# One half of each unit's sixteen small transfers moves from SyncE's queue to GpSimd's

## The chip, the cores and the metric

The kernel runs on one core of one Trainium2 chip. The metric is the time of one execution on the device in microseconds (us). Before the change the median of three runs is 1092.51 us (1091.69 to 1094.83).

## The reference

The reference is a two-layer transformer stack on 2048 tokens of 256 features. Layer 0 is a 16-head softmax attention over all 2048 tokens followed by a mixture of eight experts (two per token) beside a shared one; layer 1 is a small ReLU attention followed by a linear map. Each of the four steps stands behind a layer norm with modulation and adds into x. The change touches the softmax attention of layer 0 alone:

```
q, k, v = (x @ Wq + bq, x @ Wk + bk, x @ Wv + bv)      # 2048 x 16 heads x 16
scores  = einsum('bnhd,bmhd->bnmh', q, k) / sqrt(16)
att     = softmax(scores, axis=2)                      # over the 2048 keys
attval  = einsum('bnmh,bmhd->bnhd', att, v)
```

## The kernel before

**Units.** The attention is done in NU = 16 units: four chunks of 512 queries, and for each of them four groups of four heads. Unit u has two sides. Its maxima: for each query and head the largest score over all keys, found by TensorE (`maxima`, L627; matmuls at L634) and VectorE (`reduce_pair`, reductions at L1433). Its scores: TensorE multiplies keys with queries again (L658), ScalarE takes the exponential (L1147), and TensorE weighs the values (L689). The maximum is subtracted inside the second matmul: it is written as two float16 rows (a rounded value and its remainder, NM = 2) under the query's 48 rows in `qst`, against constant rows in `kst`. So a unit's scores can't begin before its maxima lie in `qst`.

**Order.** Each unit has MT = 16 steps t. In a step TensorE does, interleaved, the maxima of a later unit, the four scores of its own and the weighing of the step before. The maxima run LEAD = 5 steps ahead: steps 0 to 10 of unit u finish the maxima of unit u+1, steps 11 to 15 begin those of unit u+2. After step 10 VectorE takes `negative_max` (L1437) and transposes it (`turn_max`, L1444), GpSimd splits it (`split_max`, L1992: nms, nmp, nmp, the last at L1999 raises `nm_s`), and SyncE's `store_max` (L375, transfers at L383) brings it from `nmp` into `qst` in sixteen transfers of 8 rows x 32 numbers, 0.5 KB each: two halves of heads b (rows 0 to 63 and 64 to 127 of `qst`), two parts m, four blocks q. Each raises `nm_in` by 16 on landing. At the head of unit u TensorE waits for all of them (`unit`, L638). Unit 0 alone has its second half begun by ScalarE (L1125).

**SyncE's queue.** For v = 4 to 15 it does in turn: `load_q` for unit v, `move_attention(v-3)` (16 transfers, L393, after GpSimd's `gate_attention`, L2034 and L2037), waits for `nm_s`, `store_max` for unit v-1, waits until these have landed, then `zero_slots` (L417), and for v = 4 the large weight loads before it, for v = 15 `load_down` (L410). A wait in this queue holds back all that stands behind it. For v = 2 and 3 it is the same without the loads at the end. The maxima of unit 15 are stored after the loop.

**GpSimd's queue.** It adds the residual to x in two halves of eight tiles (`residual`, L2014), with `split_max(1)` between them; then for each unit `gate_attention(u)`, `split_max(u+2)`, `add_attention(u)` (L2045). Ahead of `split_max(15)` it has the work on the expert weights: `down_gated` (L2076, when `load_down` has landed) and `down_rounded` (L2103, L2105). Its indirect transfers (L2164, L2194) come after the attention.

**Other names.** `qst` has four slots, so unit v takes the slot of unit v-4. TensorE's matmuls of maxima go to two pairs of PSUM banks, and wait for VectorE's reduction of the pair before the last.

Of the kernel before, what the change touches and what calls it, by code (L numbers as in the profile page):

```python
# [21 lines left out]
TPC = CH // P  # L22
H, DH = 16, 16
G = 4
NG = H // G
NU = NC * NG
MT = T // P
HALF = 64
BLK = 3
KR = BLK * DH  # L30
NM = 2
# [3 lines left out]
GP = G // 2  # L35
LOADS = 2 * BLK
# [26 lines left out]
MI = G * TPC  # L63
QD = 32
NQ = P // QD
MAX_LOADS = 2 * NM * NQ
ROW_UNIT = 2.0 ** 15


def build(nc, x_in, wq, bq, wk, bk, wv, bv, routerT, gate_w, up_w, down_w, sg_w, sg_b, su_w, su_b,  # L70
# [18 lines left out]
    with ctx:  # L89
# [21 lines left out]
        nms, nmp = new("nms", [P, QD]), new("nmp", [P, NM, QD], F16)  # L111
# [138 lines left out]
        def sem(name):  # L250
            names[name] = ctx.enter_context(nc.semaphore(name))
            return names[name]
# [13 lines left out]
        slot_out = [sem(f"slot_out{n}") for n in range(SLOTS)]  # L266
        v_ps, v_s, vb_s, vconst = sem("v_ps"), sem("v_s"), sem("vb_s"), sem("vconst")
        kst_in = [sem(f"kst_in{g}") for g in range(3)]
        kst_one, q_in, nm_in = sem("kst_one"), sem("q_in"), sem("nm_in")
        mx_ps, mx_read, nmx_s = sem("mx_ps"), sem("mx_read"), sem("nmx_s")  # L270
        nmT_s, nm_step, nm_s = sem("nmT_s"), sem("nm_step"), sem("nm_s")
        sc_ps, p_s, pv_s, o_s = sem("sc_ps"), sem("p_s"), sem("pv_s"), sem("o_s")
# [70 lines left out]
        def _(sp):  # L343
# [28 lines left out]
                                     qd[Q_PART[r]].rearrange("(h b d) n -> b d h n", b=2, d=DH)[b][  # L372
                                         :, GP * g:GP * (g + 1), bass.ts(c, CH)]).then_inc(q_in, 16)

            def store_max(slot, halves=range(2)):  # L375

                for b in halves:
                    for m in range(NM):
                        row = HALF * b + KR + m
                        rows = qst[row:row + 1, slot, 0:GP, :].rearrange("p k (j n) -> p (k j) n", j=TPC)  # L380
                        for q in range(NQ):
                            at_ = QD * q + MI // 2 * b
                            sp.dma_start(rows[:, :, QD * q:QD * (q + 1)],  # L383
                                         nmp[at_:at_ + MI // 2, m, :]).then_inc(nm_in, 16)

            def move_attention(u, heads=range(G)):

# [59 lines left out]
            load_k(3, kst_in[2])  # L447
            store_items(EASY, max(n for which, n in FILL[:BEFORE] if which == "i") + 1)
            sp.wait_ge(nm_s, 1)
            store_max(0, (0,))  # L450
            store_items(min(n for which, n in FILL[BEFORE:] if which == "i"), len(ITEMS))
            sp.wait_ge(nm_in, 16 * MAX_LOADS)
            for v in range(2, G):
                load_q(v, 0)
                sp.wait_ge(q_in, 16 * LOADS * (v + 1))
                if v >= G - 1:
                    move_attention(v - G + 1)
                sp.wait_ge(nm_s, v)
                store_max(v - 1)
                sp.wait_ge(nm_in, 16 * MAX_LOADS * v)  # L460
            for v in range(G, NU):
                c, g = v // NG, v % NG
                if v == G:
                    stored(sp, range(len(ITEMS) - SLOTS, len(ITEMS)))
                sp.wait_ge(sc_ps, G * MT * (v - NG + 1))
                load_q(g, c)
                sp.wait_ge(q_in, 16 * LOADS * (v + 1))
                move_attention(v - G + 1)
                sp.wait_ge(nm_s, v)
                store_max((v - 1) % NG)  # L470
                sp.wait_ge(nm_in, 16 * MAX_LOADS * v)
                if v == G:
                    load_shared(ffw_in[0])
                    sp.wait_ge(vb_s, MT // 2)
                    load_gate_up(ffw_in[1])
                    sp.wait_ge(zero_s, 1)
                zero_slots(ZERO_TILES * (v - G), min(ZERO_TILES * (v - G + 1), TS))
                if v == NU - 1:
                    sp.wait_ge(sc_ps, G * MT * (NU - NG + 1))
                    load_down(ffw_in[2])  # L480
# [51 lines left out]
        def _(pe):  # L532
# [104 lines left out]

            def unit(u, g, ahead, first=False, beside=None, banks=(4, 5, 6)):  # L638

                pe.wait_ge(nm_in, (u + 1) * (16 * MAX_LOADS))  # L640
                for t in range(MT):
                    run = (t + LEAD < MI and ahead >= 1) or (t + LEAD >= MI and ahead >= 2)
                    nxt = t + LEAD < MI
                    i = (t + LEAD) % MI
                    v, vg = (u + 1, (g + 1) % NG) if nxt else (u + 2, (g + 2) % NG)
                    if run and i == 0:
                        pe.wait_ge(q_in, (u + 3) * (16 * LOADS))
                    pairs = v * (2 * MI) + 2 * i

                    def score(k):  # L650
                        n = G * t + k
                        bank = banks[n % len(banks)]
                        if n >= len(banks):
                            pe.wait_ge(p_s, u * (G * MT) + n - len(banks) + 1)
                        elif n == 0 and not first:
                            pe.wait_ge(p_s, u * (G * MT))
                        rows = slice(HALF * (k % 2), HALF * (k % 2) + KR + NM)
                        nc.tensor.matmul(ps[:, bank, :], kst[rows, GP * g + k // 2, P * t:P * (t + 1)],  # L658
                                         qst[rows, g, k // 2, :], start=True, stop=True).then_inc(sc_ps, 1)

                    def next_maxima(p):
                        if run:
                            maxima(vg, i, p, pairs + p)

                    def weigh_before(half):
                        if t == 0 and not first:
                            weigh((g - 1) % NG, MT - 1, half)
                        if t >= 1:
                            if half == 0:
                                pe.wait_ge(p_s, u * (G * MT) + G * t)  # L670
                                if t == 1 and not first:
                                    pe.wait_ge(o_s, u)
                            weigh(g, t - 1, half)

                    next_maxima(0)
                    score(0)
                    score(1)
                    weigh_before(0)
                    next_maxima(1)
                    score(2)  # L680
                    score(3)
                    weigh_before(1)
                    if beside:
                        beside(t)
# [1240 lines left out]
        def _(pool):  # L1925
# [66 lines left out]
            def split_max(v):  # L1992

                pool.wait_ge(nmT_s, v + 1)
                pool.wait_ge(nm_in, v * (16 * MAX_LOADS))
                nc.gpsimd.tensor_scalar(nms[:], nmT[:], 1.0 / ROW_UNIT, None, ALU.mult).then_inc(nm_step, 1)  # L1996
                nc.gpsimd.tensor_scalar(nmp[:, 0, :], nmT[:], 1.0 / ROW_UNIT, None, ALU.mult).then_inc(nm_step, 1)
                pool.wait_ge(nm_step, 2 * (v + 1))
                nc.gpsimd.tensor_tensor(nmp[:, 1, :], nms[:], nmp[:, 0, :], ALU.subtract).then_inc(nm_s, 1)  # L1999

            for f, (which, n) in enumerate(FILL):
# [8 lines left out]
                else:  # L2010
                    residue(n)


            def residual(lo, hi):  # L2014
                for t in range(lo, hi):
                    then(nc.gpsimd.tensor_scalar(xt[:], x[:, t, :], mv0[:, t, 0:1], rs0[:, t:t + 1],  # L2016
                                                 ALU.subtract, ALU.mult))
                    then(nc.gpsimd.tensor_tensor(xt[:], xt[:], rows0[:, GCA, :], ALU.mult))
                    then(nc.gpsimd.tensor_tensor(xt[:], xt[:], rows0[:, GSA, :], ALU.add))
                    then(nc.gpsimd.tensor_tensor(x[:, t, :], x[:, t, :], xt[:], ALU.add))  # L2020
# [19 lines left out]
            def add_attention(u):  # L2040

                c, g, w = u // NG, u % NG, G * DH
                pool.wait_ge(att_in, 16 * G * NQ * (u + 1))
                dst = x[:, c * TPC:(c + 1) * TPC, w * g:w * (g + 1)]
                nc.gpsimd.tensor_tensor(dst, dst, att_t[:].rearrange("p j k d -> p j (k d)"), ALU.add).then_inc(att_s, 1)  # L2045
# [3 lines left out]
            gates_by_head()  # L2049
            split_max(1)  # L2050
            pool.wait_ge(nm_s, 2)
            residual(NT // 2, NT)

            def zeros():
# [70 lines left out]
            for u in range(NU - 1):  # L2125
                if u == NU - 2:
                    input_rest(0)
                    tokens_by_row(0)
                    deviation(1, 1)
                gate_attention(u)  # L2130
                if u == 0:
                    zeros()
                if u == 5:
                    shared_rounded()
                if u == 6:
                    router_constants()
                    sort_tables()
                if u == NU - 3:
                    down_rounded()
                    deviation(1, 0)  # L2140
                if u + 2 < NU:
                    split_max(u + 2)
                    pool.wait_ge(nm_s, u + 3)
                add_attention(u)
                pool.wait_ge(att_s, u + 1)
                if u == NU - 4:
                    down_gated()
# [118 lines left out]
```

## Time and profile before

| | |
|---|---|
| median of three runs | 1092.51 us |
| profiled execution | 1092.85 us |
| its span | 1091.0 us |
| busy, share of the span | TensorE 87%, VectorE 78%, ScalarE 62%, GpSimd 27% |
| mean granted TensorE clock | 0.916 |
| L1433 (VectorE, maxima) | 512 reductions, 597.4 us busy, 1216 ns each |
| L1147 (ScalarE, exponentials) | 1024, 553.5 us busy, 595 ns each |

Times are of one profiled execution and count from the start of its span. PE is TensorE, PEld its weight loads, DVE VectorE, ACT ScalarE, POOL GpSimd; SPq, ACTq and POOLq are the issue of transfers by an engine. A busy TensorE is not one at its peak, since its matmuls are pipelined. The granted clock is a share of the full one, 2.4 GHz. Idle time of an engine matters where it lies in the chain that ends last.

### The profile page before, as it was taken

Reading aid. Unit: us, or ns where it says so; the run is one execution under the profiler, and the core shown is the slowest. Engines: PE = TensorE matmul, PEld = TensorE weight load, DVE = VectorE, ACT = ScalarE, POOL = GpSimd, SP = SyncE. Lnnn points to the kernel's source line nnn. Section 1 sums busy time; section 2 is a strip of 40 time slices with the busy share of each in tenths; the row PEclk is TensorE's granted clock in tenths of the full one; section 3 lists DMA queues with packets and bytes.
Section 4 is the critical chain, followed back from the end, with each engine's and each line's share of the span. In section 5 each row is a group of like instructions: output and inputs, shape, how many; then the busy total and the mean of one; then the engine's idle time right before and its main releaser. Section 6 shows DMA issues by size and latency. Waiting matters only on the chain.

```text
span 1091.0 us, 22102 instructions
## 1 busy us (share of the span) xinstructions
PE 944.5 (87%) x7744; PEld 426.7 (39%) x7744; DVE 856.0 (78%) x1204; ACT 674.9 (62%) x1300; POOL 296.8 (27%) x351
## 2 busy tenths in 40 slices
PE   4887989899899989999899898995969989797766
PEld 3442223223222222222232232222347778696545
DVE  6589979889889999899898898892537755746665
ACT  0222879779788888798797797794744334354112
POOL 2052894001000221100100010074435720314453
PEclk9999889989899998899998898898888989898888
DMA  7470000023110101001101001120001253343221
GB/s 174 120 127 30 18 9 6 13 70 110 30 27 9 30 12 25 28 6 33 28 6 33 28 6 31 37 34 2 6 6 55 81 160 99 92 135 108 59 67 58
DMA packets 90477, 54.81 MB, mean 50 GB/s; under 512 B 49334, under 2 KB 86038, under 8 KB 90390
## 3 DMA queue, kind: packets, MB, share of 16 engines
q1 hardware_dynamic: 82806, 43.52, 16.1%
q0 software_dynamic: 3072, 8.39, 2.5%
q10 hardware_dynamic: 4512, 1.67, 0.8%
q8 instruction: 63, 1.03, 0.4%
q14 instruction: 24, 0.20, 0.1%
HBM read 28.63 MB, written 22.54 MB: 47 GB/s over the span
## 4 chain that ended last, share of the span: by engine, by line
PE 29%; DVE 23%; issue 14%; SPq 13%; POOL 11%; DMA 5%; ACT 2%; ACTq 1%; DVEq 0%; POOLq 0%
DVE mxp L1433 14%; SPq L383 12%; PE ps L689 5%; PE ps L886 4%; PE ps L634 3%; PE ps L658 2%; PE ps L912 2%; DMA qst<-nmp 2%; PE ps L569 2%; POOL xt L2016 2%; PE ps L580 2%; DMA yg<-y_slots,slots 1%; PE ps L971 1%; PE ps L787 1%; DMA d_raw<-down_w 1%
## 5 line engine op out<-in xcount | busy, mean ns | idle before, releaser
L1433 DVE TENSOR_REDUCE mxp<-ps 128x2 f32<-128x1024 f32 x512 | 597.4, 1216 | 56.6 <-PE ps L634 55.4
L1147 ACT ACTIVATE prob<-ps 128x512 f32<-128x512 f32 x1024 | 553.5, 595 | 135.7 <-PE ps L658 102.9
L689 PE MATMUL ps<-prob,vp 128*32 128x256 f32 x4096 | 348.1, 414 | 14.6 <-ACT prob L1147 1.4
L634 PE MATMUL ps<-kst,qst 48*128 48x512 f16 x1024 | 211.3, 410 | 45.0 <-DMA qst<-nmp 34.8
L658 PE MATMUL ps<-qst,kst 50*128 50x512 f16 x1024 | 210.2, 404 | 10.3 <-DMA qst<-nmp 10.3
L689 PEld LDWEIGHTS ps<-prob,vp 128*32 128x32 f32 x4096 | 83.3, 111 | 202.1 <-ACT prob L1147 101.9
L634 PEld LDWEIGHTS ps<-kst,qst 48*128 48x128 f16 x1024 | 49.6, 93 | 274.4 <-issue 141.6
L658 PEld LDWEIGHTS ps<-qst,kst 50*128 50x128 f16 x1024 | 87.8, 96 | 50.6 <-ACT prob L1147 12.3
L2034 POOL TENSOR_TENSOR att_u<-o_x,rec 128x256 f32<-128x256 f32 x16 | 9.9, 620 | 255.6 <-DVE rec L1457 255.4
L1996 POOL TENSOR_SCALAR nms<-nmT 128x32 f32<-128x32 f32 x16 | 4.8, 300 | 209.8 <-DVE nmT L1444 193.7
L1690 DVE TENSOR_TENSOR hdt<-ps,sgt 128x176 f32<-128x176 f32 x46 | 15.6, 338 | 48.3 <-ACT sgt L1211 46.9
L2194 POOL DMA_INDIRECT yg<-y_slots,slots x32 | 32.1, 1002 | 51.3 <-DMA y_slots<-ysb 30.5
L1211 ACT ACTIVATE sgt<-ps 128x176 f32<-128x176 f32 x46 | 14.6, 317 | 49.4 <-PE ps L886 49.4
L886 PE MATMUL ps<-gu_hi,th 128*128 x92 | 35.8, 389 | 1.6 <-issue 1.0
L900 PE MATMUL ps<-ident,hdt 128*88 128x128 f32 x92 | 18.8, 288 | 17.3 <-DVE hl L1694 17.3
L912 PE MATMUL ps<-d_hi,hh 88*128 x92 | 31.4, 341 | 2.4 <-issue 2.4
L1319 DVE TENSOR_SCALAR xh<-x,mv,rs 128x256 f32<-128x256 f32 x56 | 20.8, 433 | 16.0 <-POOL rs L1949 12.4
L2164 POOL DMA_INDIRECT x_slots<-h_tmA,slots x24 | 26.8, 1116 | 18.4 <-DVE slots L1576 11.5
L886 PE MATMUL ps<-gu_lo,th 128*128 x92 | 30.9, 336 | 0.0
L886 PE MATMUL ps<-gu_hi,tl 128*128 x92 | 30.7, 334 | 0.0
L1217 ACT ACTIVATE hh<-ps 88x256 fp32r<-88x256 f32 x46 | 17.5, 381 | 19.0 <-PE ps L900 18.8
L1224 ACT ACTIVATE ysb<-ps 128x256 f32<-128x256 f32 x46 | 17.7, 384 | 18.4 <-PE ps L912 18.4
(271 smaller groups left out, 1151.1 us busy)
## 6 DMA issues: line engine op xcount, KB each, us to landing
xg<-x_slots SPq DMA_DIRECT2D x46, 128.0 KB, 2.1
y_slots<-ysb SPq DMA_DIRECT2D x46, 128.0 KB, 1.9
x_slots<-zero SPq DMA_DIRECT2D x10, 512.0 KB, 3.0
qst<-nmp SPq DMA_DIRECT2D x248, 0.5 KB
att_t<-att_u SPq DMA_DIRECT2D x248, 8.0 KB, 1.8
qst<-q_parts SPq DMA_DIRECT2D x96, 32.0 KB, 1.9
kst<-k_parts SPq DMA_DIRECT2D x24, 128.0 KB, 5.2
x<-x SPq DMA_DIRECT2D x4, 512.0 KB, 9.2
```

What stands on the lines that cost most here:

```text
L383: sp.dma_start(rows[:, :, QD * q:QD * (q + 1)], nmp[at_:at_ + MI // 2, m, :]).then_inc(nm_in, 16)
L569: last = nc.tensor.matmul(ps[:, 4 + n % 2, :], w[:, k, P * ft:P * (ft + 1)], hT[:, k, CH * c:CH * (c + 1)], start=k == 0, stop=k == KT - 1)
L580: last = nc.tensor.matmul(ps[:, 6 + i % 2, D * j:D * (j + 1)], hT[:, k, P * (2 * i + j):P * (2 * i + j + 1)], wv_sb[:, k, :], start=k == 0 ...
L634: last = nc.tensor.matmul(ps[:, 2 * p + b, :], qst[rows, g, a, P * j:P * (j + 1)], kst[rows, GP * g + a, CH * m:CH * (m + 1)], start=True, ...
L658: nc.tensor.matmul(ps[:, bank, :], kst[rows, GP * g + k // 2, P * t:P * (t + 1)], qst[rows, g, k // 2, :], start=True, stop=True).then_inc ...
L689: last = nc.tensor.matmul(ps[VW * k:VW * (k + 1), 7, own], vp[:, g, t, k, :], prob[:, t % 2, k, own], start=t == 0 and half == 0, stop=t = ...
L886: last = nc.tensor.matmul(ps[:, 2 + i % 2, 0:2 * I], a[:, i % 2, k, :], b[:].rearrange("p e k n i -> p (e k n i)")[:, bass.ds(e * GW + k * ...
L912: last = nc.tensor.matmul(ps[:, 6, 0:D], a[:, i % 2, n, :], b[:].rearrange("p e n d -> p (e n d)")[:, bass.ds(e * (2 * D) + n * D, D)], st ...
L1147: nc.scalar.activation(prob[:, t % 2, k, :], ps[:, banks[(G * t + k) % len(banks)], :], ACT.Exp, scale=exp_scale).then_inc(p_s, 1)
L1433: nc.vector.tensor_reduce(own, ps[:, 2 * p:2 * p + 2, :], AX.X, ALU.max).then_inc(mx_read, 1)
L2164: nc.gpsimd.indirect_dma_start(x_slots[part], bass.IndirectOffsetOnAxis(ap=slots[:, PARTS[part][0] + t, k:k + 1], axis=0), h_tm[part][:, t ...
L2194: nc.gpsimd.indirect_dma_start(yg[:, m % 4, :], None, y_slots[part], bass.IndirectOffsetOnAxis(ap=slots[:, TPC * d + j, k:k + 1], axis=0)) ...
```

## The change: what it does

`store_max` on SyncE now begins only the eight transfers of the first half (rows 48 and 49 of `qst`). GpSimd has a `store_max(v)` of its own for the second half (rows 112 and 113), right behind `split_max(v)` and its wait for `nm_s`, ahead of `add_attention` (for unit 1, ahead of the second half of the residual). Its eight raise a new semaphore, `nm_low_in`. TensorE's unit waits for both; `split_max` waits for both before it overwrites `nmp`; SyncE goes on when its own eight have landed. Unit 0 keeps ScalarE's eight. The number of transfers, their sizes and addresses stay.

```diff
-MAX_LOADS = 2 * NM * NQ
+MAX_LOADS = NM * NQ
...
-            def store_max(slot, halves=range(2)):
-                for b in halves:
-                    for m in range(NM):
-                        row = HALF * b + KR + m
...
+            def store_max(slot):
+                for m in range(NM):
+                    rows = qst[KR + m:KR + m + 1, slot, 0:GP, :].rearrange("p k (j n) -> p (k j) n", j=TPC)
+                    for q in range(NQ):
+                        sp.dma_start(rows[:, :, QD * q:QD * (q + 1)],
+                                     nmp[QD * q:QD * q + MI // 2, m, :]).then_inc(nm_in, 16)
...
-                sp.wait_ge(nm_in, 16 * MAX_LOADS * v)
+                sp.wait_ge(nm_in, 16 * MAX_LOADS * (v + 1))
...
-                pe.wait_ge(nm_in, (u + 1) * (16 * MAX_LOADS))
+                pe.wait_ge(nm_in, (u + 2) * (16 * MAX_LOADS))
+                if u:
+                    pe.wait_ge(nm_low_in, u * (16 * MAX_LOADS))
...
-                pool.wait_ge(nm_in, v * (16 * MAX_LOADS))
+                if v:
+                    pool.wait_ge(nm_in, (v + 1) * (16 * MAX_LOADS))
+                if v >= 2:
+                    pool.wait_ge(nm_low_in, (v - 1) * (16 * MAX_LOADS))
...
+            def store_max(v):
+                pool.wait_ge(q_in, 16 * LOADS * (v + 1))
+                for m in range(NM):
+                    row = HALF + KR + m
+                    rows = qst[row:row + 1, v % NG, 0:GP, :].rearrange("p k (j n) -> p (k j) n", j=TPC)
+                    for q in range(NQ):
+                        at_ = QD * q + MI // 2
+                        pool.dma_start(rows[:, :, QD * q:QD * (q + 1)],
+                                       nmp[at_:at_ + MI // 2, m, :]).then_inc(nm_low_in, 16)
...
             split_max(1)
             pool.wait_ge(nm_s, 2)
+            store_max(1)
             residual(NT // 2, NT)
...
                     split_max(u + 2)
                     pool.wait_ge(nm_s, u + 3)
+                    store_max(u + 2)
                 add_attention(u)
```

## Rows read from the trace of the kernel before

**Rows 1.** The page's part 4: the chain that ended last, by line.

```profile
DVE mxp L1433 14%; SPq L383 12%; PE ps L689 5%; PE ps L886 4%; PE ps L634 3%; PE ps L658 2%; PE ps L912 2%; DMA qst<-nmp 2%; PE ps L569 2%; POOL xt L2016 2%; PE ps L580 2%; DMA yg<-y_slots,slots 1%; PE ps L971 1%; PE ps L787 1%; DMA d_raw<-down_w 1%
```

**Rows 2.** Waits of PE: us in total, times, longest; 200 to 703, then the span.

```profile
PE ps L634 <- DMA qst<-nmp: 27.7, 12, 2.7
...
PE ps L658 <- DMA qst<-nmp: 10.3, 1, 10.3
```

**Rows 3.** Timeline (start, us, [idle before <- releaser]): POOL, then SP, before unit 4.

```profile
310.97 0.29 POOL L1996 TENSOR_SCALAR nms<-nmT 128x32 f32<-128x32 f32 x1 [17.65 <-DVE nmT L1444]
...
311.59 0.25 POOL L1999 TENSOR_TENSOR nmp<-nms,nmp 128x32 f16<-128x32 f32 x1
...
311.87 10.79 SPq L383 DMA_DIRECT2D qst<-nmp  x16
```

**Rows 4.** Timeline of PE at the head of unit 4.

```profile
321.02 0.64 PE L689 MATMUL ps<-prob,vp 128*32 128x256 f32 x8
323.76 0.61 PE L634 MATMUL ps<-kst,qst 48*128 48x512 f16 x2 [2.10 <-DMA qst<-nmp]
```

**Rows 5.** Timeline of DVE, unit 3 and the head of unit 4.

```profile
291.66 18.72 DVE L1433 TENSOR_REDUCE mxp<-ps 128x2 f32<-128x1024 f32 x16
310.42 0.22 DVE L1437 TENSOR_REDUCE nmx<-mxp 128x16 f32<-128x64 f32 x1
...
310.81 11.37 DVE L1433 TENSOR_REDUCE mxp<-ps 128x2 f32<-128x1024 f32 x10
324.41 1.23 DVE L1433 TENSOR_REDUCE mxp<-ps 128x2 f32<-128x1024 f32 x1 [2.23 <-PE ps L634]
...
327.85 0.72 DVE L1453 STREAM_TRANSPOSE o_x<-ps 128x512 f32<-128x512 f32 x1 [0.24 <-PE ps L689]
```

**Rows 6.** Windows of unit 4: us, busy time (instructions) by engine, granted clock, DMA share.

```profile
323.70:331.70 8.00, 7.90 (x52) 1.52 (x52) 5.61 (x6) 4.34 (x8) 0.00 (x0) 0.59 0.33 92
331.70:366.00 34.30, 31.49 (x332) 9.90 (x332) 32.77 (x31) 30.39 (x56) 2.86 (x6) 1.00 0.05 5
```

**Rows 7.** Timeline of POOL's indirect transfers, and DVE beside the first.

```profile
840.10 2.11 POOL L2164 DMA_INDIRECT x_slots<-h_tmA,slots  x1 [0.30 <-DVE h32a L1504]
...
880.12 0.96 POOL L2164 DMA_INDIRECT x_slots<-h_tmB,slots  x1 [0.30 <-issue]
...
839.76 1.61 DVE L1625 TENSOR_TENSOR gu_lo<-gu_raw,gu_hi 128x1408 fp32r<-128x1408 f32 x1
```

**Rows 8.** DMA issues: count, KB each, median us to landing; span, span, then 238 to 256.

```profile
x_slots<-h_tmA,slots POOLq DMA_INDIRECT x24, 2.4
...
qst<-q_parts SPq DMA_DIRECT2D x96, 32.0 KB, 1.9
...
qst<-q_parts SPq DMA_DIRECT2D x6, 32.0 KB, 2.9
```

**Rows 9.** Timeline before unit 2: POOL, SP, PE.

```profile
173.57 0.73 POOL L2037 TENSOR_TENSOR att_u<-att_u,ga_q 128x256 f32<-128x256 f32 x1
...
174.37 10.60 SPq L393 DMA_DIRECT2D att_t<-att_u  x16
185.02 10.82 SPq L383 DMA_DIRECT2D qst<-nmp  x16
...
196.90 0.48 PE L634 MATMUL ps<-kst,qst 48*128 48x512 f16 x2 [2.57 <-DMA qst<-nmp]
```

**Rows 10.** The chain in order of time before unit 15 (start, us), then PE's timeline.

```profile
690.83 0.71 SPq L383
...
703.61 12.19 DMA d_raw<-down_w
715.93 8.88 POOL d_raw L2076
...
741.16 0.70 SPq L383
...
753.05 0.61 PE L658 MATMUL ps<-qst,kst 50*128 50x512 f16 x2 [10.25 <-DMA qst<-nmp]
```

More of the change, by code:

```diff
@@ L268, in build @@
         kst_in = [sem(f"kst_in{g}") for g in range(3)]
-        kst_one, q_in, nm_in = sem("kst_one"), sem("q_in"), sem("nm_in")
+        kst_one, q_in, nm_in, nm_low_in = sem("kst_one"), sem("q_in"), sem("nm_in"), sem("nm_low_in")
         mx_ps, mx_read, nmx_s = sem("mx_ps"), sem("mx_read"), sem("nmx_s")
@@ L373, in load_q @@
                                          :, GP * g:GP * (g + 1), bass.ts(c, CH)]).then_inc(q_in, 16)
-            def store_max(slot, halves=range(2)):
-                for b in halves:
-                    for m in range(NM):
-                        row = HALF * b + KR + m
[L380 to L384, printed above, removed]
+            def store_max(slot):
[4 more added lines that the diff above has]
+                                     nmp[QD * q:QD * q + MI // 2, m, :]).then_inc(nm_in, 16)
             def move_attention(u, heads=range(G)):
@@ L449, in _ @@
             sp.wait_ge(nm_s, 1)
-            store_max(0, (0,))
+            store_max(0)
             store_items(min(n for which, n in FILL[BEFORE:] if which == "i"), len(ITEMS))
-            sp.wait_ge(nm_in, 16 * MAX_LOADS)
+            sp.wait_ge(nm_in, 16 * MAX_LOADS * 2)
             for v in range(2, G):
@@ L470, in _ @@
                 store_max((v - 1) % NG)
-                sp.wait_ge(nm_in, 16 * MAX_LOADS * v)
+                sp.wait_ge(nm_in, 16 * MAX_LOADS * (v + 1))
                 if v == G:
```

## The prediction

> **What bounds the kernel now.** I read the page's chain of waits first, because the busy shares can't tell which of four half-busy engines sets the end. The chain has VectorE's reductions of maxima at 14% and, right behind, SyncE issuing the small transfers (L383) at 12% [rows 1]: some 130 us in which the end waits for nothing but issue. The second view is the list of waits: between 200 and 703 TensorE stands 27.7 us in 12 waits for these transfers, 2.3 us each, at the heads of units 3 to 14, and once 10.3 us at the head of unit 15 [rows 2].
>
> The third view is the timeline around one such head, unit 4. GpSimd's last split ends at 311.84, SyncE issues sixteen transfers in 10.79 us (0.674 us apart, the last beginning at 321.98) [rows 3], and TensorE starts the unit at 323.76 [rows 4]. From the split to the start that is 11.92 us, of which 1.78 us lie behind the start of the last transfer. TensorE's work of the unit before ended at 321.66 [rows 4]. So the transfers have a **budget** of 321.66 - 311.84 = 9.82 us in which they cost nothing, and they overrun it by 2.1 us here. VectorE sees the same hole as 2.23 us [rows 5].
>
> The hole costs more than its length. In the 8 us behind it the granted clock is 0.59, so most of them at the lower level of 1.2 GHz; in the remaining 34.3 us it is 1.00 [rows 6]. At the low clock TensorE doesn't keep VectorE fed.
>
> What comes next if the hole goes? VectorE's own work of a unit: 32 reductions at 18.72/16 = 1.17 us are 37.4, the small maximum and its transposition put 0.39 between two reductions (310.42 to 310.81), the transposition of the output 0.72, its wait 0.24 [rows 5]: 38.8, and I take 38.9 us, for the reciprocal and seams. The unit takes 366.0 - 323.7 = 42.3 [rows 6]. **At most 3.4 us a unit can be had**: 2.1 of hole, 1.3 of slow clock. Then VectorE is the bound.
>
> **The change part by part.**
>
> *SyncE's half.* Eight issues go from its queue: 8 x 0.674 = 5.4 us. Its own eight are in place 7 x 0.674 + 1.78 = 6.5 us after the split, 3.3 inside the budget. The waits on other semaphores have the same meaning and cost nothing.
>
> *GpSimd's half.* The trace shows no plain transfer begun by GpSimd. Call the distance between two of them p, and L the time from the start of the last to its landing: the half is in place after 0.1 + 7p + L (0.1 for the two semaphore waits, as between 311.84 and 311.87 on SyncE, rounded up). The nearest row is GpSimd's indirect transfer: 0.96 us and a gap of 0.30 ahead of it, p = 1.26 [rows 7]; it lands after 2.4 us [rows 8]. From below, SyncE's 0.674 for the same transfer: were GpSimd quicker still, SyncE's half would be the last, so less brings no more. From above, the slowest indirect transfer, 2.11 + 0.30 = 2.41 [rows 7]. I take p = 1.1: the gap whole, and 0.8 of the 0.96, since eight rows of 64 bytes have to be described and not 128 rows. L is 2.4: the landing writes less, but shares the engines, as told below. So the half needs 0.1 + 7.7 + 2.4 = 10.2 us, 0.4 over the budget.
>
> Only a page has a price for the plain transfer: the Trainium skill, "DMA: Bandwidth & Descriptors", section "Latency and other measured facts", gives about 1 us to the first byte where GpSimd's software writes the descriptors and about 0.6 where hardware does; SyncE's 0.674 is near the second, the first is shown by no run here. By 1.0 for p, an estimate from that page, the half would fit the budget and the sum would come to about 1051 us.
>
> *Heads of units 3 to 13, eleven of them.* Each loses 3.4 us but keeps 0.4 of hole, on which I count no fall of the clock: 11 x (3.4 - 0.4) = 33.0 us gained (the slow stretch of unit 13 is in it, which lies ahead of the split for unit 14).
>
> *Neighbours.* SyncE goes on when its own half has landed, at 6.5 us, and then begins 0.5 MB of zeros and six loads of queries, which before came behind the last maximum. They now run beside GpSimd's last transfers. Loads of queries take 2.9 us to land beside heavy traffic and 1.9 otherwise [rows 8]; the 2.4 in L has part of that. At the head of unit 3, where the weights of the experts are loaded, I add 1 us once.
>
> *Ahead of unit 2.* GpSimd's eight issues for unit 1 push the second half of the residual back by 8p = 8.8 us. That half is not covered: gate_attention follows it and ends at 174.30, SyncE's move_attention begins at 174.37 and takes 10.6 us, and only behind that come the maxima of unit 2 at 185.02 [rows 9]. So SyncE's queue is 8.8 us late and then 5.4 us shorter: unit 2 starts 3.4 us later. That unit 1 starts sooner helps nothing, since unit 2 waits for this queue. TensorE waited 2.57 here [rows 9]; this hole grows.
>
> *Ahead of unit 15.* Here GpSimd is the chain: SyncE's store for unit 14 (690.83), load_down landing for 12.19 us behind its issue, GpSimd's 8.88 us on it and the rest up to 741.16, and the store for unit 15, 11.9 us up to 753.05 [rows 10]. load_down waits for SyncE's half alone and so begins 5.4 us sooner; GpSimd's own eight are done by then. The last store takes 10.2 and not 11.9. Together 7.1 us gained, and TensorE, which waited 10.25 us, still waits.
>
> *Covered by GpSimd's idle time.* In units 2 to 13 its eight issues (8.8 us) stand ahead of add_attention, and behind that GpSimd waits about 17 us and more for VectorE [rows 3]. If this cover went, move_attention would come late, as ahead of unit 2.
>
> *Sum.* +3.4 - 33.0 + 1.0 - 7.1 = -35.7 us. The profiled execution took 1092.85 us (span 1091.0, 1.85 around it), 0.3 above the median of 1092.51. 1092.85 - 35.7 = **1057 us**.
>
> **The rivals.**
>
> *GpSimd pays the price of its indirect transfers.* With p = 1.26 and L = 2.4 the half needs 11.3 us, and 1.5 of the hole stay: 0.8 x 11 = 8.8 gained at the heads, 4.7 lost ahead of unit 2, 5.4 + 0.6 gained ahead of unit 15, 10 in all: 1083, if the clock still falls; with the clock kept, 14 less, 1069. For it speaks that this is the one measured row of GpSimd's queue; against it that those transfers have sixteen times as many rows.
>
> *GpSimd's half becomes the later one than all sixteen were: slower.* The place is the same eight issues, ahead of every head and ahead of the residual. All terms together change by 92 us for one us of p (8 ahead of unit 2, 77 at the heads, 7 at unit 15), and with L = 2.4 they are zero at p = 1.37. At p = 1.5 and L = 2.6 the half takes 13.2 us: +6.6, +1.1 x 11, -5.4 + 1.3, together +15: 1108. For it: p = 1.37 is only 0.11 above the indirect row. Against it: eight rows instead of 128.
>
> *VectorE holds GpSimd up.* One indirect transfer took 2.11 us while VectorE ran a subtraction with both inputs in SBUF (from 839.76) [rows 7]. At p = 2.41 the half takes 19.4 us, the holes grow by 7.3 x 11, unit 2 starts 13.9 later, unit 15's stage loses 2.1: about 1189. Against it: in the 12 us behind a split VectorE does ten reductions out of PSUM and nothing else [rows 5]. The Trainium skill, "SBUF — State Buffer", section "Who interferes with whom", says that a VectorE instruction in certain modes shuts GpSimd out of writing descriptors, and that a reduction never does; by that rule this rival falls, and no run here has shown it yet.
>
> *A small hole still lets the clock fall.* Then 1.3 x 11 = 14 us come back: 1071. The hole of 2.1 us ahead of unit 4 is followed by the slow stretch [rows 6]; a hole of 0.4 us I don't have to read.
>
> **How the numbers follow.** The forecast, with p up to about 1.15, has 0.52; its own range is 1044 (p as on SyncE: 37.4 + 10.8 gained, nothing lost ahead of unit 2) to 1064. The indirect price or the falling clock, 1064 to 1089, has 0.28. No gain, 1089 to 1096, has 0.05; the slow GpSimd 0.12; VectorE's hold 0.03. The range 1042 to 1090 leaves out the last three and a little at the low end, about 0.2. Some 0.3% (3.3 us) is what a measurement of this kernel can tell from no change: faster 0.80, same 0.05, slower 0.15.
>
> **What would show it.** In the profile after: L383 with half its count, on POOL eight transfers behind L1999 some 1.1 us apart; TensorE's waits for the maxima at the heads of units 3 to 14 near zero, the granted clock at 1.00 through them, and a unit of about 39 us; move_attention(0) beginning some 9 us later, near 183; d_raw landing 5.4 us sooner behind the split for unit 14. It is wrong where GpSimd's transfers stand 1.3 us apart or more, where the unit stays above 41 us, or where GpSimd's own queue turns up in the chain of units 3 to 13.

## The result, and the profile after

The changed kernel takes 1041.41 us (median of four runs, 1040.90 to 1042.52); beside it the kernel before took 1092.1. The ratio is 0.9548, with a 95% interval of 0.95 to 0.9595. Ratios here are taken over the fast runs and not from the medians, which leaves out one run of the kernel before beside e1, e2, e3 and e5, and two of e9's six, its profiled one (1038.83) among them. The forecast of 1057 had the sign and the mechanism, but the gain is 51 us and not 36. The median lies 0.6 us under the low end of the wide range, 1042 to 1090 (0.9548 of the 1092.51 that the prediction started from is 1043.1, just inside it), and under the 1044 at which the forecast's own range began. The profiled execution took 1042.52 us (span 1040.7).

The chain that ended last, from the page of the changed kernel, answers to [rows 1]. SyncE's line of the small transfers (12% before) is gone from the list, and VectorE's has fallen from 14% to 3%; TensorE and ScalarE stand there in turn:

```profile
PE ps L688 14%; ACT prob L1146 13%; PE ps L631 8%; PE ps L657 7%; PE ps L885 4%; DVE mxp L1432 3%; PE ps L566 2%; PE ps L911 2%; PE ps L577 2%; PE ps L970 1%; PE ps L786 1%; DMA yg<-y_slots,slots 1%; PE ps L541 1%; SPq L390 1%; DVE x L1745 1%
```

TensorE's waits for the maxima over the whole span (us in total, times, longest) answer to [rows 2]: only the heads of unit 2 and of unit 15 are left.

```profile
PE ps L631 <- DMA qst<-nmp: 6.2, 1, 6.2
...
PE ps L657 <- DMA qst<-nmp: 3.0, 1, 3.0
```

The timelines behind one split (GpSimd, then SyncE) answer to [rows 3]. Under them stand GpSimd's eight per unit as a group (ns: shortest, median, longest; first and last start) and the landing of the transfers out of nmp, us from issue (shortest, median, longest), which the trace has for GpSimd's:

```profile
303.69 0.25 POOL L2001 TENSOR_TENSOR nmp<-nms,nmp 128x32 f16<-128x32 f32 x1
304.23 4.17 POOL L2024 DMA_DIRECT2D qst<-nmp  x8 [0.30 <-POOL nmp L2001]
...
303.96 5.44 SPq L380 DMA_DIRECT2D qst<-nmp  x8
...
L2024 POOL DMA_DIRECT2D qst<-nmp x120: 497/518/824, 143.6 to 699.0; - x120
...
DMA to landing us min/median/max: 1.5/1.9/2.9
```

GpSimd's transfers stand 4.17/8 = 0.52 us apart and were forecast at 1.1. GpSimd's half is in place 0.3 + 7 x 0.52 + 1.9 = 5.8 us behind the split, SyncE's half 6.5, both far inside the budget of 9.8.

The windows of one unit (us, busy time by engine, granted clock, DMA share, GB/s) answer to [rows 6]: 38.57 us and not 42.3, the clock at 1.00 throughout.

```profile
264.57:303.14 38.57, 36.76 (x388) 11.45 (x384) 38.19 (x37) 34.67 (x66) 7.04 (x15) 1.00 0.11 24
```

Ahead of unit 2 (GpSimd, SyncE, TensorE) nothing is won and nothing lost; the rows answer to [rows 9]:

```profile
178.69 0.73 POOL L2050 TENSOR_TENSOR att_u<-att_u,ga_q 128x256 f32<-128x256 f32 x1
...
179.50 10.93 SPq L390 DMA_DIRECT2D att_t<-att_u  x16
190.47 5.46 SPq L380 DMA_DIRECT2D qst<-nmp  x8
...
196.99 0.61 PE L631 MATMUL ps<-kst,qst 48*128 48x512 f16 x2 [6.17 <-DMA qst<-nmp]
```

Ahead of unit 15 (SyncE, GpSimd, SyncE, TensorE), answering to [rows 10], the way from SyncE's store for unit 14 to TensorE's start has shrunk from 62.2 us (690.83 to 753.05) to 50.9 (651.06 to 701.94):

```profile
651.06 5.45 SPq L380 DMA_DIRECT2D qst<-nmp  x8
...
658.00 1.08 SPq L407 DMA_DIRECT2D d_raw<-down_w  x2
...
669.89 8.89 POOL L2090 TENSOR_TENSOR d_raw<-d_raw,rows 88x4096 f32<-88x4096 f32 x1 [13.64 <-DMA d_raw<-down_w]
...
695.16 5.45 SPq L380 DMA_DIRECT2D qst<-nmp  x8
...
701.94 0.39 PE L657 MATMUL ps<-qst,kst 50*128 50x512 f16 x2 [3.03 <-DMA qst<-nmp]
```

**Where the 50.3 us of span came from.** Up to the start of unit 2: +0.1 (196.90 to 196.99). From there to the store for unit 14: 493.9 before, 454.1 now, -39.9. From that store to the start of unit 15: -11.3. From there to the end: 338.0 before, 338.8 now, +0.8.

### The profile page after: what moved, and what is told of

Same layout as the page of the kernel before. It is cut to its first block, busy times and chain, and to the rows that moved or that the text cites. A ratio compares the mean times of both kernels' runs of the same rounds, so it can differ in the third digit from the quotient of the medians.

```text
span 1040.7 us, 22104 instructions
## 1 busy us (share of the span) xinstructions
PE 917.2 (88%) x7744; PEld 427.6 (41%) x7744; DVE 852.5 (82%) x1204; ACT 674.3 (65%) x1300; POOL 358.8 (34%) x471
## 4 chain that ended last, share of the span: by engine, by line
PE 49%; ACT 14%; issue 12%; DVE 12%; POOL 7%; DMA 2%; SPq 1%; ACTq 1%; DVEq 0%; POOLq 0%
PE ps L688 14%; ACT prob L1146 13%; PE ps L631 8%; PE ps L657 7%; PE ps L885 4%; DVE mxp L1432 3%; PE ps L566 2%; PE ps L911 2%; PE ps L577 2%; PE ps L970 1%; PE ps L786 1%; DMA yg<-y_slots,slots 1%; PE ps L541 1%; SPq L390 1%; DVE x L1745 1%
## 5 line engine op out<-in xcount | busy, mean ns | idle before, releaser
L688 PE MATMUL ps<-prob,vp 128*32 128x256 f32 x4096 | 333.4, 398 | 23.1 <-ACT prob L1146 10.0
L631 PE MATMUL ps<-kst,qst 48*128 48x512 f16 x1024 | 202.4, 393 | 16.6 <-DVE mxp L1432 10.4
L657 PE MATMUL ps<-qst,kst 50*128 50x512 f16 x1024 | 201.6, 387 | 6.7 <-ACT prob L1146 3.7
L2024 POOL DMA_DIRECT2D qst<-nmp x120 | 62.8, 531 | 4.5 <-POOL nmp L2001 4.5
```

Source lines behind the costliest of these rows:

```text
L631: last = nc.tensor.matmul(ps[:, 2 * p + b, :], qst[rows, g, a, P * j:P * (j + 1)], kst[rows, GP * g + a, CH * m:CH * (m + 1)], start=True, ...
L688: last = nc.tensor.matmul(ps[VW * k:VW * (k + 1), 7, own], vp[:, g, t, k, :], prob[:, t % 2, k, own], start=t == 0 and half == 0, stop=t = ...
L2024: pool.dma_start(rows[:, :, QD * q:QD * (q + 1)], nmp[at_:at_ + MI // 2, m, :]).then_inc(nm_low_in, 16)
```

## The experiments

The budget theory says that the transfers cost only what they overrun the time between the split and the end of TensorE's work, and the slow clock behind the hole. The rivals were that every transfer taken from SyncE is worth the same, or that GpSimd's share matters for itself. e1 to e5 and e8 differ from the change only in which engine begins which transfer, or in cutting some transfers in two, with `ALL_STORES` the sixteen in the order of the kernel before. This table has the median times (e4, e6 and e10 have a single run each; the kernel before took 1092.2 to 1093.4 beside the experiments), and from each profile the start of unit 15 and what lies between it and the end of the span (us):

| | time | unit 15 starts | from there to the end |
|---|---|---|---|
| before | 1092.1 | 753.05 | 338.0 |
| the change (8 + 8) | 1041.4 | 701.94 | 338.8 |
| e1, 12 + 4 | 1054.6 | 708.59 | 345.8 |
| e2, 14 + 2 | 1061.8 | 716.26 | 347.6 |
| e3, SyncE's cut in two | 1075.9 | 729.47 | 346.3 |
| e4, GpSimd's cut in two | 1079.9 | 729.81 | 348.3 |
| e5, units 14 and 15 alone | 1082.0 | 736.16 | 344.1 |
| e6, half reductions | 1036.1 | 696.58 | 337.7 |
| e7, store first | 1035.3 | 695.23 | 340.2 |
| e8, 0 + 16 | 1056.5 | 715.47 | 340.4 |
| e9, load_down early too | 1032.5 | 690.12 | 346.9 |
| e10, half maxima | 1014.9 | 673.06 | 340.0 |

The last column moves by 10 us among kernels whose code behind the attention is the same. So each experiment is judged by the middle column and the units, not by the time alone; I come back to it. The middle column has a spread of its own: the first small maximum, ahead of all that was changed, starts between 97.3 and 100.7 us in the profiles whose maxima are whole.

**e1: twelve on SyncE, four on GpSimd.**

```diff
-SyncE: ALL_STORES[:8]     GpSimd: ALL_STORES[8:]
+SyncE: ALL_STORES[:12]    GpSimd: ALL_STORES[12:]
```

> SyncE keeps twelve of the sixteen transfers, GpSimd takes four. Budget theory (the transfers cost only what they overrun the 9.82 us between the split and the end of TensorE's work, and the slow clock behind that): twelve on SyncE are in place after 0.05 + 11 x 0.674 + 1.78 = 9.2 us, inside the budget, so the heads of units 3 to 13 keep their whole gain (41 us in the changed kernel); unit 2 starts 0.3 sooner than before the change, load_down 2.7 sooner, the last store 2.7 shorter: some 46 us under the kernel before, 1046, and no waits at those heads. Rival (each transfer taken off SyncE is worth the same share of the 50 us): 4/8 of it, 25 us, 1067.

Windows of one unit, and the head in it (TensorE's timeline):

```profile
266.75:305.34 38.59, 36.66 (x386) 11.46 (x384) 38.19 (x37) 34.68 (x65) 5.02 (x11) 1.00 0.10 24
...
277.18 0.39 PE L655 MATMUL ps<-kst,qst 48*128 48x512 f16 x2 [0.38 <-DMA qst<-nmp]
```

Half as many transfers moved, and the unit is the same 38.6 us: this is the budget theory, and the rival of equal worth (1067) falls. Ahead of unit 15 the way is 55.9 us (652.7 to 708.6), 5.0 longer than in the change, where 5.4 was expected. Unit 15 starts 44.5 us sooner than before, for 46 forecast. The time itself, 1054.6 (ratio 0.9649, 0.9584 to 0.9714), misses 1046 by 8.6 us, 7 of which are in the last column; these belong to neither of the two theories.

**e2: fourteen and two.**

```diff
+SyncE: ALL_STORES[:14]    GpSimd: ALL_STORES[14:]
```

> SyncE keeps fourteen, GpSimd takes two. Budget theory: 0.05 + 13 x 0.674 + 1.78 = 10.6 us, a hole of 0.8 us at the heads of units 3 to 14. If so small a hole leaves the clock at its upper level: 41 - 0.8 x 11 = 32 gained there, 2.7 ahead of unit 15: 1057. If the clock falls behind it as behind the holes of 2.1 us, 1.3 x 11 more is lost: 1071. Rival (same worth for each transfer): 2/8 of 50, 12 us, 1080.

One unit, the head in it, and the 8 us behind that head:

```profile
305.10:344.10 39.00, 36.66 (x388) 11.38 (x387) 38.19 (x37) 34.68 (x65) 4.00 (x9) 1.00 0.11 24
...
315.92 0.39 PE L655 MATMUL ps<-kst,qst 48*128 48x512 f16 x2 [0.79 <-DMA qst<-nmp]
...
315.90:323.90 8.00, 7.23 (x76) 2.21 (x76) 7.51 (x7) 6.22 (x12) 0.00 (x0) 1.00 0.31 92
```

The hole is 0.79 us, as worked out, and the clock stays at its upper level behind it. Three of the twelve heads have more, 1.23 to 1.45 us, and behind these too the clock is 1.00. The unit grows by 0.4 and not by 0.8: half of so small a hole is taken back. Unit 15 starts 36.8 us sooner than before, for 35 forecast in the time; the time, 1061.8 (ratio 0.9712, 0.9658 to 0.9766), is 4.8 over the 1057, with 8.9 us more in the last column than the change has.

**e3: SyncE's eight cut in two, GpSimd's as in the change.**

```diff
+SyncE: in_two(ALL_STORES[:8])    GpSimd: ALL_STORES[8:]
+# in_two: (b, m, q) as rows 0 to 3 and rows 4 to 7
```

> GpSimd does its eight as in the change; SyncE's eight are each cut into two of half the rows, so that it issues sixteen again, of half the bytes. Budget theory with a fixed price per issue: SyncE's share is again in place after 11.9 us, all holes are back, the residual is still 4.5 us late ahead of unit 2, load_down gains nothing: 1092 + 4 = 1097. If the issue goes by rows and not by transfers, or if the gain came from GpSimd's share alone, the time stays at that of the change, 1041 to 1043.

SyncE's sixteen, two heads, and the 8 us behind each of these heads:

```profile
271.95 9.93 SPq L404 DMA_DIRECT2D qst<-nmp  x16
...
282.93 0.39 PE L655 MATMUL ps<-kst,qst 48*128 48x512 f16 x2 [1.90 <-DMA qst<-nmp]
323.16 0.39 PE L655 MATMUL ps<-kst,qst 48*128 48x512 f16 x2 [1.26 <-DMA qst<-nmp]
...
282.90:290.90 8.00, 7.91 (x68) 2.04 (x72) 6.82 (x7) 5.51 (x11) 0.00 (x0) 0.79 0.29 92
323.10:331.10 8.00, 7.20 (x76) 2.22 (x76) 7.47 (x7) 6.18 (x12) 0.00 (x0) 1.00 0.31 92
```

Half the rows cost 0.62 us each where the whole cost 0.67: SyncE's price is nearly one per transfer. GpSimd's share is in place early, and the holes are back nevertheless: 1.26 us at most heads, with units of 39.45, and behind the one of 1.90 the clock falls. It also falls, to 0.58, behind one of 1.56 (unit 13, which takes 41.7 us), but not behind one of 1.58 (unit 10). The rival that GpSimd's share brings the gain (1041 to 1043) falls. The time is 1075.9 (0.9851, 0.98 to 0.9901), not the 1097 expected: I had put the price at the full 0.674 and the hole at 2.1. With 0.62 the same sum gives 0.05 + 15 x 0.62 + 1.78 = 11.1 us and a hole of 1.3, and most holes of 1.3 don't bring the slow clock.

**e4: GpSimd's eight cut in two, SyncE's as in the change.**

```diff
+SyncE: ALL_STORES[:8]    GpSimd: in_two(ALL_STORES[8:])
```

> The change, with each of GpSimd's eight transfers cut into two of half the rows; SyncE's eight as they are. If GpSimd's price is one per transfer, they stay 0.52 us apart, the share is in place after 0.3 + 15 x 0.522 + 1.9 = 10.0 us, 0.2 over the budget, and units stay at 38.6 to 38.7 us, with unit 2 some 3 us later: 1043 to 1050. If the price goes by rows, they stand 0.26 us apart and the time is that of the change, 1041.

GpSimd's group and its landing, as above, its timeline at the ninth burst, and TensorE's waits at the heads, whose releaser the profile doesn't name:

```profile
L2049 POOL DMA_DIRECT2D qst<-nmp x240: 497/518/824, 143.5 to 728.1; - x120
...
DMA to landing us min/median/max: 1.5/1.9/7.7
...
474.67 8.25 POOL L2049 DMA_DIRECT2D qst<-nmp  x16 [3.40 <-issue]
...
PE ps L655 <- issue: 24.1, 13, 6.0
```

Four rows cost what eight cost, 0.52 us: one price per transfer here too. But units 3 to 13 are 38.8 to 42.6 us, the way ahead of unit 15 is 59.3 us (670.5 to 729.8) against 50.9 in the change, and the time is 1079.9 (a single run), far over the 1043 to 1050 forecast. GpSimd's last transfers are now issued when SyncE, whose half was in place at 6.5 us, has begun its zeros and loads. At the heads of units 4 to 6 the slowest of them lands 2.9 to 3.2 us after its issue, where the sum had 1.9; at unit 14, beside load_down, the last three take 6.9 to 7.7 us, and the head waits 6.0 us. In the change no landing takes over 2.9 us: GpSimd is done before SyncE goes on. This looks like the neighbours' term that the prediction feared; that the traffic is the cause is read from the order of the transfers, and no run here moves SyncE's zeros and loads alone. The burst for unit 9 began 3.4 us late for another reason, told below.

**e5: the change for units 14 and 15 alone.**

```diff
+SyncE:  ALL_STORES[:8] if w >= NU - 2 else ALL_STORES
+GpSimd: ALL_STORES[8:] if w >= NU - 2 else []
```

> The change for the stores of units 14 and 15 alone; units 1 to 13 are stored as before. Budget theory with load_down as a term of its own: load_down begins 5.4 us sooner, the last store is 5.4 us shorter, the hole ahead of unit 14 goes: about 11 to 14 us, 1079 to 1082. Rival (all stores alike): 2/15 of 50 us, 7 us, 1085.

```profile
736.16 0.61 PE L681 MATMUL ps<-qst,kst 50*128 50x512 f16 x2 [3.36 <-DMA qst<-nmp]
```

That is TensorE's head of unit 15. SyncE's store for unit 14 began at 684.9, so the way is 51.2 us, against 62.2 before and 50.9 in the change: the 11 us ahead of unit 15 are a term of their own, load_down and the shorter last store. The time, 1082.0 (0.9899, 0.987 to 0.9929), is 10 us under the kernel before, at the upper end of the 1079 to 1082 expected.

**e6 and e10: is VectorE the bound of the changed kernel?** e6 reduces only half of each bank; e10 also computes only that half.

```diff
-nc.vector.tensor_reduce(own, ps[:, 2 * p:2 * p + 2, :], AX.X, ALU.max)
+nc.vector.tensor_reduce(own, ps[:, 2 * p:2 * p + 2, 0:CH // 2], AX.X, ALU.max)
...
-kst[rows, GP * g + a, CH * m:CH * (m + 1)]          # e10
+kst[rows, GP * g + a, CH * m:CH * m + CH // 2]
```

> The change, with VectorE's reductions of maxima reading only half of each bank (256 of 512 columns), so that half of the keys are left out of the maxima. If VectorE's reductions are what sets the changed kernel's unit of 38.57 us, the unit falls to what ScalarE's 64 exponentials need, 64 x 0.54 = 34.6 us or a little more, and the run is about 45 us shorter, 990 to 1000. If it is the round of TensorE and ScalarE that the chain of waits names, the unit stays at 38.5 and the time at 1041.

> As the run with half the reductions (unit 38.30 us), and TensorE's matmuls of maxima take only 256 of each 512 keys too, so that half of the maxima's work is left out on both engines. If the round of TensorE and ScalarE that the chain of waits names (weigh 0.64, maxima 0.32, scores 0.26, exponential 0.60 and the gaps: 2.35 us a step) sets the unit, each step loses about half of the 0.32 and the unit falls by 16 x 0.1 to 0.16, to 35.7 to 36.7 us; ScalarE's 64 exponentials alone need 34.6. If it is something else (the number of waits, ScalarE's own queue), it stays at 38.3.

One unit of e6, then one of e10:

```profile
300.50:338.80 38.30, 36.75 (x388) 11.46 (x384) 23.27 (x36) 34.67 (x65) 7.04 (x14) 1.00 0.11 24
```

```profile
291.90:328.60 36.70, 34.43 (x388) 10.31 (x384) 23.25 (x36) 34.62 (x65) 7.04 (x14) 1.00 0.12 25
```

VectorE's work fell from 38.2 to 23.3 us a unit and the unit by 0.3: VectorE was not the bound, or at most by these 0.3. With half of the matmuls gone too the unit falls to 36.7. The chain of waits in order of time (start, us) shows why, first the change, then e10, one step each:

```profile
280.79 0.60 ACT prob L1146
281.39 0.04 issue
281.44 0.64 PE ps L688 x8
282.07 0.32 PE ps L631 x2
282.40 0.26 PE ps L657 x2
...
282.79 0.35 issue
283.14 0.60 ACT prob L1146
```

```profile
281.45 0.60 ACT prob L1146
282.05 0.04 issue
282.09 0.64 PE ps L688 x8
282.73 0.21 PE ps L631 x2
282.95 0.26 PE ps L657 x2
...
283.35 0.35 issue
283.69 0.60 ACT prob L1146
```

A step is one round of TensorE and ScalarE: exponential, weighing, maxima, scores, next exponential. It takes 2.35 us in the change and 2.24 in e10, and the maxima's part of it went from 0.32 to 0.21. The 16 steps of a unit at 0.11 each are 1.8 us, and the unit fell by 1.6 from e6 to e10. Two reductions of 1.17 us fill the same 2.35 by coincidence.

**e7 and e9: what the profile after points to.** e7 stores unit 2's maxima ahead of move_attention(0). e9 also begins load_down ahead of SyncE's wait for unit 14's maxima, and puts GpSimd's deviation of the layer norm behind the store for unit 15 (the old place of load_down and the move of the deviation are not in the lines shown).

```diff
 sp.wait_ge(q_in, 16 * LOADS * (v + 1))          # v = 2, 3
-if v >= G - 1:
-    move_attention(v - G + 1)
 sp.wait_ge(nm_s, v)
 store_max(v - 1)
+if v >= G - 1:
+    move_attention(v - G + 1)
...
 move_attention(v - G + 1)                       # e9, v = 4 to 15
+if v == NU - 1:
+    sp.wait_ge(sc_ps, G * MT * (NU - NG + 1))
+    load_down(ffw_in[2])
 sp.wait_ge(nm_s, v)
```

> The change, and in SyncE's queue for v = 3 alone the store of unit 2's maxima ahead of move_attention(0) (before, they wait behind its sixteen transfers, and TensorE waits 6.2 us at the head of unit 2). Theory: the maxima of unit 2 are then in place 6.5 us behind the split, before TensorE has ended unit 1; the hole of 6.2 us and some 1 us of slow clock go: 7 us under the change, 1034. Rival: the later move_attention(0) holds GpSimd (add_attention, then gate_attention(1)) and the 7 us come back at the heads of units 3 and 4: 1041.

> As the one before, and ahead of unit 15: load_down begins before SyncE's wait for the maxima of unit 14 and not behind their store, and GpSimd splits and stores unit 15's maxima before the deviation of the layer norm. Theory (GpSimd's work on the expert weights is what unit 15's store waits for): it is done some 13 us sooner, the split waits for VectorE alone, and the hole of 3.0 us at the head of unit 15 shrinks to under 1: 2 to 3 us under the kernel before it, 1031 to 1032. Rival: the deviation, now behind the store, holds back the transposition at the end of unit 14, and nothing is gained: 1034.

SyncE's timeline of e7; then of e9 GpSimd's on the weights and TensorE's head of unit 15:

```profile
182.15 5.34 SPq L380 DMA_DIRECT2D qst<-nmp  x8
187.53 11.43 SPq L390 DMA_DIRECT2D att_t<-att_u  x16
```

```profile
647.43 8.88 POOL L2090 TENSOR_TENSOR d_raw<-d_raw,rows 88x4096 f32<-88x4096 f32 x1
...
690.12 0.39 PE L657 MATMUL ps<-qst,kst 50*128 50x512 f16 x2
```

e7 loses the hole of unit 2 and starts unit 15 at 695.23, 6.7 us sooner than the change. e9 has no wait for maxima left from unit 2 on and starts it at 690.12, 11.8 us sooner. Of the 5.1 us between the two, 1.6 are there at the first small maximum (98.8 against 100.4); the rest is e7's hole of 3.6 ahead of unit 15. The times are 1035.3 (ratio 0.9473, 0.9429 to 0.9518) and 1032.5 (0.9413, 0.9365 to 0.9462). e9's interval lies under that of the change, 0.95 to 0.9595: of the full computations it is the fastest. Whether it beats e7 by more than chance the intervals leave open, and which of e9's two moves counts was not tried.

**e8: all sixteen on GpSimd.**

```diff
+SyncE: []    GpSimd: ALL_STORES
```

> GpSimd begins all sixteen transfers of units 1 to 15, SyncE none. Budget theory with the distance of 0.52 us read from the changed kernel: in place after 0.3 + 15 x 0.522 + 1.9 = 10.0 us, 0.2 over the budget, so units of 38.6 to 39.0 us; unit 2 no longer waits behind SyncE's queue and starts 2 to 3 us sooner, unit 15 about 2 us later: 1040 to 1045. Rival (a longer burst on GpSimd's queue slows down, or the gain comes from two queues working at once): units of 40 us and more, 1058 and over.

TensorE's head of unit 3, and GpSimd's burst for unit 9:

```profile
237.97 0.61 PE L655 MATMUL ps<-kst,qst 48*128 48x512 f16 x2 [2.81 <-issue]
...
464.54 8.24 POOL L2049 DMA_DIRECT2D qst<-nmp  x16 [3.40 <-issue]
```

Most units are 38.57 us, as forecast for 10.0 us at the brink of the budget, and a burst of sixteen is no slower per transfer; so the gain doesn't need two queues at once. The time of 1056.5 (0.9672, 0.9627 to 0.9718) missed 1040 to 1045. Two units are 42.93: unit 3's maxima landed beside the weights of the experts, which SyncE no longer held back (3.0 to 5.0 us from issue), and the burst for unit 9 began 3.4 us late. And unit 14's maxima landed beside load_down (3.2 to 6.9 us), its head waited 4.5 us, and the way from the split for unit 14 to unit 15 is 57.1 us, 6 more than in the change.

## Why the prediction was nearly right

**The budget.** Right, and shown by e1 to e3 and most heads of e8: a store in place within some 9.8 us costs nothing, whoever issues it, and an overrun of 0.8 or 1.3 us is the hole that TensorE shows.

**The distance p between GpSimd's transfers.** This is the term that was mis-sized: 0.52 us where I took 1.1, and under the lower of my ends, 0.674 and 2.41. I took SyncE's 0.674 as the lower end because less would bring no more, which held at the heads; but I chose by the nearest row of the same queue, the indirect transfer, and scaled only its busy part by its rows. With p = 0.52 and L = 1.9 the prediction's own sum is 8 x 0.52 - 5.4 = -1.2 ahead of unit 2, -37.4 at the heads and -5.4 - 5.4 ahead of unit 15: -49.4 and 1043.4, without the 1 us for neighbours. That this is 0.9 from the profiled 1042.5 is partly luck: the stages measured +0.1, -39.9 and -11.3, with +0.8 behind them, so that errors of up to 2.5 us cancel. The Trainium skill, "DMA: Bandwidth & Descriptors", section "Latency and other measured facts", gives about 1 us to the first byte of a transfer that GpSimd issues, which is a latency and not a distance. The 1.0 that I took from it as an estimate of p was nearer to the measured 0.52 than my 1.1, and still twice it.

**The heads of units 3 to 13.** 38.9 us a unit was forecast without a hole, 38.57 measured; I had left 0.4 us of hole that wasn't there. The hole is p again, and L, which measured 1.9 where I took 2.4; the 0.3 of the unit is in the next point.

**"Then VectorE is the bound."** Wrong, though the number fitted. I added up VectorE's work and took a full engine for the limit; e6 took 15 us of work a unit from it and the unit fell by 0.3. That its sum of 38.8 came near the unit is luck: the round of TensorE and ScalarE was the limit, which the chain of the changed kernel names and e10 bears out.

**Ahead of unit 2.** The mechanism held: residual, move_attention, store, in that order. gate_attention ended 5.1 us later and not 8.8, and SyncE's queue became 5.4 shorter: 0.1 in place of +3.4. e7 shows that this queue was the cause of the hole.

**Ahead of unit 15.** 11.3 us gained, 7.1 forecast. With p and L as measured the forecast is 10.8, and e5 has the term alone.

**The neighbours.** Nothing of the 1 us came: GpSimd's half was in place at 5.8 us and SyncE went on at 6.5. Where transfers of GpSimd were still under way beside SyncE's loads (e4, e8), the term was larger than I had put it.

**The clock.** That a small hole leaves it alone held in e1 to e4. At the heads of units 3 to 14 the granted clock of the next 8 us was 1.00 behind every hole up to 1.45 us, and 0.57 to 0.79 behind every hole from 1.90 us on, the kernel before among them. Holes of 1.54 to 1.60 us went both ways. A hole of 0.4 us itself occurred only once (0.38 in e1, clock 1.00).

**VectorE's hold on GpSimd.** None: no transfer of GpSimd out of nmp took over 0.82 us in the change, with VectorE at its reductions beside the bursts. This agrees with what the Trainium skill, "SBUF — State Buffer", section "Who interferes with whom", says of reductions.

## What to carry to other kernels

Small transfers ahead of a barrier have a time budget, and only the overrun counts; measure from the last input to the end of the consumer's earlier work before counting transfers. A hole's price can include what the clock does behind it: here holes up to 1.45 us left it alone and holes from 1.90 us on did not, so shrinking them gave more than their length. What is in place in time can be undone by the traffic that it meets on its way (e4, e8). An engine that is busy all the time isn't shown to be the limit until its work is made smaller.

## What the runs showed that was not expected

GpSimd's plain transfer costs 0.52 us for eight rows of 64 bytes and the same for four; SyncE's 0.67 and 0.62. For such small transfers GpSimd's queue was the quicker one to issue.

After 128 transfers GpSimd stood still once: 3.40 us ahead of the 129th in e4 and in e8 (the burst of unit 9 in both), with nothing in the trace that held it. In the change the 129th is the ninth indirect transfer, and it too stands out, 1.18 us where its neighbours have 0.30. So it does in e3, e6, e7, e9 and e10, which also begin 120 small ones (1.16 to 1.18), and in none of the kernel before, e1, e2 and e5, which begin fewer, or e4 and e8, where the ninth indirect one is not the 129th (0.30 or 0.31 in all). The count is what these have in common; what the 129th waits for stays open:

```profile
786.91 0.97 POOL L2179 DMA_INDIRECT x_slots<-h_tmA,slots  x1 [0.30 <-issue]
789.06 0.95 POOL L2179 DMA_INDIRECT x_slots<-h_tmA,slots  x1 [1.18 <-issue]
```

Behind the attention, where nothing was changed, the profiles differ by up to 10 us. In e1 the granted clock there is 0.92 over 40 us (windows from 80 us behind the start of unit 15), in the change 1.00:

```profile
788.60:828.60 40.00, 33.81 (x195) 28.95 (x194) 25.99 (x44) 12.68 (x18) 32.49 (x27) 0.92 0.25 86
```

```profile
782.00:822.00 40.00, 36.31 (x217) 30.03 (x216) 30.05 (x47) 13.45 (x20) 30.00 (x26) 1.00 0.23 80
```

Why the clock falls in one and not in the other wasn't tried. The times of e7 (1029.75 to 1042.39) and e9 (1023.24 to 1038.83) spread wider than those of the change; their mean clock over a whole run goes with it (in e7 0.960 in the shortest run and 0.948 in the longest), but that it is this stretch is not shown. This is why a step of a few us in the attention is read from the start of unit 15.
